# Sorted rows that carry their experts' shares, weighting moved into the expert tiles, and gathers that add to the residual

## The reference, cut to what matters

```
x = x + L0_attn(layernorm(x))
x = x + wkv(w, u, layernorm(x), ctx)
x = x + experts(layernorm(x))
x = x + L1_attn(layernorm(x))
x = x + cross_attention(layernorm(x), ctx)
x = x + mlp(layernorm(x))

experts(h):
    logits = h @ router_weight.T + router_bias
    top_vals, top_idx = top_k(logits, 2)
    top_w = softmax(top_vals)                    # the two shares of a token
    expert_out[e] = down(e, glu(gate_up(e, h)))
    out = sum over the two chosen experts of top_w * expert_out
```

## Time and profile before

| | |
|---|---|
| time, median of three runs | 3035.04 us (3031.03 to 3040.39) |
| the profiled execution: time, span | 3033.89 us, 3032.2 us |
| busy share: PE, DVE, ACT, POOL | 91%, 82%, 64%, 70% |
| mean granted clock of PE | 0.956 |

### The profile page before, as it was taken

One profiled execution on the slowest core, in us unless ns is written; L12 is line 12 of the kernel. 1 busy time (PEld: TensorE's weight loads), 2 busy tenths in 40 slices (PEclk: granted clock), 3 DMA queues, 4 the chain that ended last, 5 costly groups with the idle time before them and its releaser, 6 DMA issues. The chain is left out here.

```text
span 3032.2 us, 68140 instructions
## 1 busy us (share of the span) xinstructions
PE 2750.8 (91%) x22096; PEld 2295.9 (76%) x22128; DVE 2487.2 (82%) x5452; ACT 1954.2 (64%) x4120; POOL 2111.9 (70%) x2651
## 2 busy tenths in 40 slices
PE   6999999999999999999788499667999999999978
PEld 3888888888888888888555299535777777777767
DVE  6888888888888888888599577468899898989863
ACT  5888878778787877878444155346666666666642
POOL 5897666666666666666468544369888989898870
PEclk9999999999999999999899699768999999999989
DMA  4555444444444444444444399600000000000000
GB/s 144 172 193 169 133 143 139 144 135 146 137 131 153 131 143 132 155 131 128 142 152 146 134 337 333 207 15 18 20 19 27 21 25 24 22 24 22 21 5 11
DMA packets 185881, 340.09 MB, mean 112 GB/s; under 512 B 40668, under 2 KB 104037, under 8 KB 178936
## 3 DMA queue, kind: packets, MB, share of 16 engines
q1 hardware_dynamic: 179448, 319.55, 32.6%
q0 software_dynamic: 6144, 16.79, 1.8%
HBM read 264.68 MB, written 63.19 MB: 108 GB/s over the span
## 5 line engine op out<-in xcount | busy, mean ns | idle before, releaser
L1804 POOL TENSOR_TENSOR l_prod<-l_sco,l_kv 128x256 f32<-128x256 f32 x512 | 369.5, 760 | 36.4 <-DVE l_sco L2311 36.4
L1797 POOL TENSOR_TENSOR l_prod<-l_q,l_kv 128x256 f32<-128x256 f32 x512 | 358.9, 743 | 47.3 <-DVE l_att L2319 47.3
L718 DVE SCALAR_TENSOR_TENSOR a_cq<-a_PQ,a_taps,a_cq 128x504 f32<-128x504 f32 (+2 forms) x384 | 281.7, 734 | 72.7 <-ACT a_cq L584 63.6
L718 DVE SCALAR_TENSOR_TENSOR a_ck<-a_PK,a_taps,a_ck 128x504 f32<-128x504 f32 (+2 forms) x384 | 280.6, 731 | 9.7 <-ACT a_ck L584 0.5
L342 POOL TENSOR_TENSOR a_tq<-a_cq,a_tq 128x512 f32<-128x512 f32 x128 | 165.9, 1296 | 131.2 <-ACT a_tq L590 131.1
L329 POOL TENSOR_TENSOR a_hrs<-a_hve,a_neghalf 128x8 f32<-128x8 f32 x128 | 209.6, 1638 | 25.7 <-DVE a_hve L735 25.2
L485 PE MATMUL a_Y<-a_wo,a_og_parts 128*128 128x256 f32 x1536 | 205.9, 284 | 5.0 <-POOL a_og_parts L336 5.0
L412 PEld LDWEIGHTS a_X<-a_wv,a_xb 128*128 128x128 f32 x1536 | 200.0, 188 | 12.1 <-issue 1.2
L342 POOL TENSOR_TENSOR a_tk<-a_ck,a_tk 128x512 f32<-128x512 f32 x128 | 163.6, 1278 | 62.8 <-ACT a_tk L590 62.8
L412 PE MATMUL a_PQ<-a_x_hi,a_wqk 128*128 (+1 forms) x512 | 194.1, 420 | 12.6 <-issue 11.9
L412 PE MATMUL a_X<-a_wv,a_xb 128*128 128x256 f32 x1536 | 204.2, 282 | 0.8 <-DMA a_xb<-a_x_lo 0.8
(11 more groups left out here) (398 smaller groups left out, 8380.6 us busy)
## 6 DMA issues: line engine op xcount, KB each, us to landing
a_wqk<-qk_parts SPq DMA_DIRECT2D x112, 512.0 KB, 3.4
m_wgu<-gate_up_parts SPq DMA_DIRECT2D x39, 1024.0 KB, 8.1
a_wv<-v_parts SPq DMA_DIRECT2D x56, 512.0 KB, 3.8
a_wg<-g_parts SPq DMA_DIRECT2D x112, 256.0 KB, 3.3
a_wo<-o_parts SPq DMA_DIRECT2D x112, 256.0 KB, 2.9
a_dr<-decays SPq DMA_DIRECT2D x256, 64.0 KB, 2.6
m_hs<-sorted_rows SPq DMA_DIRECT2D x39, 256.0 KB, 7.1
sorted_outs<-m_ys SPq DMA_DIRECT2D x39, 256.0 KB, 7.5
```

Source lines behind the costliest of these rows:

```text
L718: nc.vector.scalar_tensor_tensor(out=acc, in0=src, scalar=taps[p][:, tap + k:tap + k + 1], in1=acc, op0=ALU.mult, op1=ALU.add).then_inc(s_ ...
L1797: nc.gpsimd.tensor_tensor(out=prod[:, h], in0=qv[:, h:h + 1, :].to_broadcast([P, H, HD]), in1=kk, op=ALU.mult).then_inc(S("E_pqk"), 1)
L1804: nc.gpsimd.tensor_tensor(out=prod[:, h], in0=sco[:, h:h + 1, :].to_broadcast([P, HD, H]), in1=vv, op=ALU.mult).then_inc(S("E_pav"), 1)
```

## The change

1. A sorted row has 259 numbers instead of 256 (1036 bytes instead of 1024). Behind the normed token stand the number of its first expert, its SHARE (the second expert's) and MORE (what the first expert has over that). `choose` writes the first with one copy more, `settle` the others with four small operations instead of three. `settle(r)` stands directly behind `place(r)` at the end of the same step, the last one ahead of `tile_table`, and `scatter` waits for it.
2. In the tile phase DVE works out the share of each of the 256 rows of a tile with two operations on 128x2: `first_choice` (1 or 0 times MORE) ahead of rows_low, `shares` (plus SHARE) behind it. ACT multiplies the result rows in m_ys by it (`weigh`, two activations of 128x256) at the end of its loop, one tile later. m_ys has three buffers, and the store waits for ACT and is issued one iteration later.
3. In `layer_one` the three small operations of the gather, the buffers got and `combine` go. Each of the two indirect DMAs adds its rows straight to x_sb; `gather(0)` is issued in a new stage G0, one iteration ahead of `gather(1)`, which waits until the first one's rows for the same tile have landed.

```diff
@@ recurrence_and_experts: a sorted row's width, buffers
+    FIRST_EXPERT, MORE, SHARE, WIDE = D, D + 1, D + 2, D + 3
+        xh, w0 = some(2, "xh", [P, BT, WIDE]), sb("w0", [P, BT])
-            hs = own_some(4, "hs", [P, 2, D])
+            hs = own_some(4, "hs", [P, 2, WIDE])
+            pick, w_of = own_some(2, "pick", [P, 2]), own_some(8, "w_of", [P, 2])
-            LOADS, STORES = 4, 2
+            LOADS, STORES = 4, 3
@@ SP
                 def load(i):
                     if i >= LOADS:
                         sp.wait_ge(S("x_hT"), i - LOADS + 1)
+                        sp.wait_ge(S("x_share"), i - LOADS + 1)
...
                 def store(i):
-                    sp.wait_ge(S("x_y"), i + 1)
+                    sp.wait_ge(S("x_ys"), 2 * i + 2)
...
-                for i in range(-3, N + 1):
-                    if i >= 1:
-                        store(i - 1)
+                for i in range(-3, N + 2):
+                    if i >= 2:
+                        store(i - 2)
@@ POOL
                 def scatter(b, part=slice(0, 2 * BT)):
                     pool.wait_ge(S("slot"), b + 1)
                     pool.wait_ge(S("xh"), 4 * b + 4)
+                    pool.wait_ge(S("carried"), 3 * b + 3)
@@ ACT
+                def weigh(i):
+                    act.wait_ge(S("x_share"), i + 1)
+                    act.wait_ge(S("x_y"), i + 1)
+                    for h in range(2):
+                        nc.scalar.activation(ys[i % STORES][:, h, :], ys[i % STORES][:, h, :], ACT.Identity,
+                                             scale=w_of[i % 8][:, h:h + 1]).then_inc(S("x_ys"), 1)
@@ DVE
                     nc.vector.tensor_copy(ixf[:, b * BT:(b + 1) * BT, :], ix8[:, :, 0:2]).then_inc(S("ixf"), 1)
+                    nc.vector.tensor_copy(xh[b % 2][:, :, FIRST_EXPERT], ix8[:, :, 0]).then_inc(S("carried"), 1)
...
-                    own_w = wts[:, b * BT:(b + 1) * BT, :]
-                    nc.vector.reciprocal(own_w[:, :, 0], te[:, 2, :]).then_inc(S("w0"), 1)
+                    nc.vector.reciprocal(w0[:], te[:, 2, :]).then_inc(S("w0"), 1)
                     dve.wait_ge(S("w0"), b + 1)
-                    nc.vector.tensor_tensor(out=own_w[:, :, 1], in0=own_w[:, :, 0], in1=te[:, 1, :], op=ALU.mult).then_inc(S("w1"), 1)
+                    share, more = xh[b % 2][:, :, SHARE], xh[b % 2][:, :, MORE]
+                    nc.vector.tensor_tensor(out=share, in0=w0[:], in1=te[:, 1, :], op=ALU.mult).then_inc(S("carried"), 1)
+                    dve.wait_ge(S("carried"), 3 * b + 2)
+                    nc.vector.tensor_tensor(out=more, in0=w0[:], in1=share, op=ALU.subtract).then_inc(S("carried"), 1)
...
-                    if r:
-                        settle(r - 1)
...
                     if r is not None:
                         place(r)
+                        settle(r)
                 tile_table()
-                settle(BLOCKS - 1)
...
+                def first_choice(i):
+                    dve.wait_ge(S(f"x_in{i % LOADS}"), 16 * (i // LOADS + 1))
+                    row = hs[i % LOADS]
+                    nc.vector.scalar_tensor_tensor(out=pick[i % 2][:], in0=row[:, :, FIRST_EXPERT], scalar=who[:, i:i + 1],
+                                                   in1=row[:, :, MORE], op0=ALU.is_equal, op1=ALU.mult).then_inc(S("x_pick"), 1)
+                def shares(i):
+                    dve.wait_ge(S("x_pick"), i + 1)
+                    if i >= 8:
+                        dve.wait_ge(S("x_ys"), 2 * (i - 8) + 2)
+                    nc.vector.tensor_tensor(out=w_of[i % 8][:], in0=pick[i % 2][:], in1=hs[i % LOADS][:, :, SHARE],
+                                            op=ALU.add).then_inc(S("x_share"), 1)
@@ layer_one
-    FIRST = dict(G=-2, Dn=-1, D=0, Dt=1, En=1, E=2, Et=3, F=4, Ft=5, M=7, Md=8)
+    FIRST = dict(G0=-3, G=-2, Dn=-1, D=0, Dt=1, En=1, E=2, Et=3, F=4, Ft=5, M=7, Md=8)
...
-            def gather(t):
-                wait_if(pool, S("G_ready"), 2 * t)
-                wait_if(pool, S("G_x"), 2 * t)
-                nc.gpsimd.tensor_tensor(out=ready[:], in0=neghalf[:, 0:1], in1=neghalf[:, 0:1], op=ALU.mult).then_inc(S("G_ready"), 1)
-                nc.gpsimd.tensor_copy(of_tile[:], slots[:, tile(t), :].rearrange("p t k -> p (t k)")).then_inc(S("G_at"), 1)
...
-                for k in range(2):
-                    nc.gpsimd.indirect_dma_start(got[k][:], None, outs[:, :],
-                                                 bass.IndirectOffsetOnAxis(ap=of_tile[:, k:k + 1], axis=0)).then_inc(S(f"G_in{k}"), 16)
+            def gather(k):
+                def piece(t):
+                    if k:
+                        pool.wait_ge(S("G_in0"), 16 * t + 16)
+                    nc.gpsimd.indirect_dma_start(x_sb[:, t, :], None, outs[:, :], bass.IndirectOffsetOnAxis(ap=slots[:, t, k:k + 1], axis=0),
+                                                 compute_op=ALU.add).then_inc(S(f"G_in{k}"), 16)
+                return piece
...
-                           ("G", gather)])
+                           ("G", gather(1)), ("G0", gather(0))])
...
-            def combine(t):
-                for k in range(2):
-                    dve.wait_ge(S(f"G_in{k}"), 16 * t + 16)
...
-                    nc.vector.scalar_tensor_tensor(out=row(t), in0=got[k][:], scalar=wts[:, tile(t), k:k + 1].rearrange("p t k -> p (t k)"),
-                                                   in1=row(t), op0=ALU.mult, op1=ALU.add).then_inc(S("G_x"), 1)
...
-                          ("M", m_hidden(0)), ("D", d_rope), ("Dn", combine), ("Et", et_values(0)), ("Ft", divide("F", MI)),
-                          ("Dn", statistics("D", "G_x", 2)), ("F", f_x2lo), ("Dt", d_x), ("M", m_hidden(1)),
+                          ("M", m_hidden(0)), ("D", d_rope), ("Et", et_values(0)), ("Ft", divide("F", MI)),
+                          ("Dn", statistics("D", "G_in1", 16)), ("F", f_x2lo), ("Dt", d_x), ("M", m_hidden(1)),
```

More of the change, by code:

```diff
@@ L783, in _, with recurrence_and_experts @@
             dve.wait_ge(s_yout, 2 * BLOCKS)
-def recurrence_and_experts(nc, new_sem, x_sb, ident, slots, wts, rows, outs, bias_rows, gu_parts, w_gu, w_down, b_experts, w_router, b_router,
+def recurrence_and_experts(nc, new_sem, x_sb, ident, slots, rows, outs, bias_rows, gu_parts, w_gu, w_down, b_experts, w_router, b_router,
                            ctx_in, wu_cols, w_kv, b_cross, kvd):
@@ L833, in recurrence_and_experts @@
         who_i, where_i = (sb(n, [P, SLOT_TILES], mybir.dt.int32) for n in ("who_i", "where_i"))
-        zeros, ends = sb("zeros", [P, D]), sb("ends", [P, E], mybir.dt.int32)
+        zeros, ends = sb("zeros", [P, WIDE]), sb("ends", [P, E], mybir.dt.int32)
         sems = {}
@@ L841, in S @@
             return sems[name]
-        xh = some(2, "xh", [P, BT, D])
+        xh, w0 = some(2, "xh", [P, BT, WIDE]), sb("w0", [P, BT])
         with ExitStack() as rounds:
@@ L861, in own_some @@
                 return [own(f"{name}{i}", shape, dt) for i in range(n)]
[L863 removed]
+            hs = own_some(4, "hs", [P, 2, WIDE])
+            pick, w_of = own_some(2, "pick", [P, 2]), own_some(8, "w_of", [P, 2])
             hT = own_some(2, "hT", [P, 2, DC, ROWS], F32R)
             gp, th, ur = (own_some(2, n, [P, DC, ROWS]) for n in ("gp", "th", "ur"))
[L866 removed]
+            aT, ys = own_some(2, "aT", [P, 2, DC, ROWS], F32R), own_some(3, "ys", [P, 2, D])
             past = [v[:].rearrange("p s t -> p (s t)")[:, 0:2 * TILES * E].rearrange("p (n e) -> p n e", e=E) for v in (eh, ev)]
@@ L911, in _ @@
                 sp.dma_start(rows[E * ROOM:E * ROOM + ROWS, :].rearrange("(h p) d -> p h d", p=P),
-                             zeros[:].unsqueeze(1).to_broadcast([P, 2, D])).then_inc(S("filled"), 16)
+                             zeros[:].unsqueeze(1).to_broadcast([P, 2, WIDE])).then_inc(S("filled"), 16)
                 for b in range(BLOCKS):
@@ L1257, in normalise @@
                     for j in range(BT):
-                        nc.scalar.activation(out[:, j, :], x_sb[:, b * BT + j, :], ACT.Identity, bias=nm[k][:, j:j + 1],
+                        nc.scalar.activation(out[:, j, 0:D], x_sb[:, b * BT + j, :], ACT.Identity, bias=nm[k][:, j:j + 1],
                                              scale=rs[k][:, j:j + 1]).then_inc(S(done), 1)
@@ L1360, in aT_out @@
                     nc.scalar.activation(aT[i % 2][:, 0], ur[i % 2][:], ACT.Copy).then_inc(S("x_aTe"), 1)
-                for i in range(-3, N):
+                def weigh(i):
[4 more added lines that the diff above has]
+                                             scale=w_of[i % 8][:, h:h + 1]).then_inc(S("x_ys"), 1)
+                for i in range(-3, N + 1):
                     if i + 3 < N:
@@ L1369, in _ @@
                         up_out(i + 2)
+                    if i >= 1:
+                        weigh(i - 1)
             @block.vector
@@ L1598, in _ @@
                     if i + 3 < N:
+                        first_choice(i + 3)
                         rows_low(i + 3)
```

(12 more changed lines are left out.)

6 lines of the change are left out of this document (removed).

## The result

The changed kernel takes 3095.66 us (median; 3089.79 to 3102.44), the kernel before in the same session 3033.03: a ratio of 1.0209, 95% interval 1.0187 to 1.023. It is slower by 2.1%, and outside the range of 3030 to 3066. The profiled execution took 3092.37 us with a span of 3090.6.

The account below looks back on a forecast made before the run. The prediction took PE to bound the tile phase and a DVE-PE loop of 29.98 us layer one's turns. 5.6 + 1.1 + 2.5 - 1.5 = +7.7 us on 3033.89 gave 3042 us, range 3030 to 3066.

Parts of the forecast that it names:

- the steady turns: Layer one's full pipeline turns: removing POOL's small operations and combine only lengthens existing waits; 0, at most -1 us.
- The turn's bound: Layer one: DVE's 9.96 us from et_x to l_oD, PE's 19.87 and a handover make a turn of 29.98 us.
- experiment of its own: Layer one, earlier trace: the turn from 2845.20 to 2875.19, without gather or combine, is as long as the others.
- Rounds, +5.6: Rounds: the scatter waits 0.7 us longer, for settle, in each of eight places; +5.6 us.
- The bound of +7.2: Rounds: upper limit of the cost of settle ahead of the scatter, 8 x 0.9 us.
- Wide rows, "cost 0": Tile phase: rows 12 bytes wider cost 0, since DMA has some 10% to spare.
- the end of the tile phase: The last store goes out after ACT's part of the last tile, and layer one waits for it; +1.1 us.
- the start of layer one: Tile 0's second gather waits for the first one's rows, delaying the statistics; +2.5 us, between -0.3 and +5.6.
- DVE's and ACT's additions in the tile phase: Per tile, DVE's 0.2 to 0.4 us and ACT's 1.04 us fit within PE's 4.73 us.
- the rival: Layer one: adding gathers are dear on POOL, deciding from 0.4 us more each; middle +22 us, 3063; chance 0.13.
- Filling, -1.5: Layer one's pipeline filling: a shorter gather on POOL saves time in five turns; -1.5 us, bounds 0 and -4.
- the lock: Tile phase: DVE's shares is held up by POOL's act_low in each tile; +40 us, 3081; chance 0.11.

Follow-up runs that it names:

- The two fillers: Changed kernel with DVE work written to a spare buffer in combine's place: two two-input operations, 3073.25 us (1.0104), or four one-input reductions, 3123.61 us (1.0315).

## Why the prediction was wrong

*The step that failed is that of the steady turns*: "0 (at most -1 in all, from fewer meetings of DVE and POOL)". The turn's bound was right: it is 29.97 us as soon as f_x2lo is out of the way, and neither the gather nor combine was on it. But the step asked only who waits for the removed instruction, not what stands behind it on its engine and when that now starts. In the kernel before combine itself waited for the product that POOL was at (56 of its 64 operations took 0.75 us or more, the other eight 0.47 to 0.49), and what stood behind it kept step with POOL: in most full turns l_x started 0.09 us ahead of a product's end and took 0.41. In the changed kernel it starts elsewhere in a product, most often 0.26 to 0.28 us ahead of its end. The two fillers show that it was this and not combine's length: in full turns l_x starts 4.25 and 4.33 us behind their start, almost alike, but 0.09 us ahead of a product's end with the one and mostly 0.34 with the other. Why l_x then waits in one turn to the end of the product that runs (0.55 us) and in another, from almost the same start, to the end of all sixteen (4.65), the traces don't show. The moment is not all of it: in the kernel before without combine, in a turn of the filling, an l_x that started 0.09 us ahead of a product's end took 3.81.

The "experiment of its own" was one turn, in which l_x took 0.65 us. Two turns on, still without combine, the same trace has the 2.84 us that stand as the longest in the view of before above. One turn in which nothing happened was taken for a rule; a view by tile of all 32 would have warned.

*Rounds, +5.6*: that the scatter starts later and holds up POOL's power functions behind it was right, the term was mis-sized: the seven places of the rounds cost 15.5 us in place of 4.9. Settle's own 0.7 us a place is there. The sum has nothing for the handover of 0.80 in place of 0.28 us, nor for the scatters that take longer beside DVE's work, and it held that nothing comes back where settle had stood, while there DVE's scan moved forward to the third DMA. Together they make 11.3 us as an edit by itself. Nor did it ask what PE's clock does when its waits move: 0.88 for 0.92 in the first five steps, 0.87 for 1.00 in the pair of runs without down_low. From one execution to another the same code's rounds took 187.7 to 191.1 us. The bound of +7.2 took no account of any of this.

*Wide rows, "cost 0"*: right for the tiles, which is where it was looked for, wrong at the phase's start, where the last zero fills and scatters are waited for: about +4 in the traces.

*Right*: the end of the tile phase (the last store 1.71 us behind the result in place of 0.72, +1.0 for +1.1) and the start of layer one (+2.6 from there to the statistics, for +2.5); DVE's and ACT's additions in the tile phase, hidden as said; and that the gathers would fit on POOL. They are dearer by 0.6 us each, more than the 0.4 from which the rival was to decide, but from the first one's start to the end of l_rsF it is 4.22 us, where the old gather with its three small operations took 4.17.

*Filling, -1.5*: not found. With f_x2lo moved, layer one takes 1077.8 to 1083.8 us in four traces with the change, and 1079.5 and 1081.2 in two without: what is sought is less than they differ among themselves, so this stays open.

*The rivals*: the lock was named, with its place in the tile phase, where it didn't come; it came in layer one. The rule of the Trainium skill cited there (SBUF — State Buffer, Who interferes with whom) has the loser wait for the one instruction that holds the pair. Here the measurement goes further: l_x waited through seven products in a row, and once through nine (6.30 us).
